# Edge chunks of seven in place of four in a four-layer graph network on one core

## The reference

```python
# conv: batch norm over the edges, gate and update, sum by dst
z = concat([h[src], h[dst], edge]);  gate = sigmoid(bn(z @ W_int + b_int));  upd = softplus(bn(z @ W_upd + b_upd))
conv = softplus(h + bn(segment_sum(gate * upd, dst)))
# sage: mean of the neighbours
sage = (segment_sum(h[src], dst) / deg) @ w_l.T + h @ w_r.T + b
# hops, three times: a mask for every edge from both its ends, then a masked sum by src
a = relu([relu(x[src] @ nb_W), relu(x[dst] @ self_W)] @ att1_W + b);  mask = clip(sigmoid(a @ att2_W) * 1.5 - 0.45, 0, 1)
d = clip(rowsum(mask) ** -0.5, 0, 10);  x = segment_sum(mask * d[src] * d[dst] * x[dst], src);  out += x
# classifier: message of node and edge, mean by dst, layer norm
msg = relu([h[src], edge] @ W1 + b1) @ W2 + b2;  out = layernorm(h + segment_sum(msg, dst) / deg)
```

## Time and profile before

| | us |
|---|---|
| median of 3 runs | 15924.5 (15921.29 to 15934.76) |
| the profiled execution | 15891.89 |
| its span | 15890.3 |
| PE, DVE, ACT, POOL busy | 8863.8, 7549.7, 6748.7, 5861.8 |
| stages in their order: placing, conv spread, statistics, messages | 3215, 967, 1034, 1099 |
| sage's sum; first masks; first hop; one spread | 742; 863; 747; 240 |
| classifier's spread; its sum | 446; 715 |

### The profile page before, as it was taken

How to read it: one execution, slowest core, us unless ns; L and a number is a source line. 1 busy time by engine, 2 the same in 40 slices (tenths; PEclk the granted TensorE clock), 3 DMA queues, 4 the chain that set the end, 5 groups by cost and what they waited for, 6 DMA issues and landing times. The chain is left out here.

```text
span 15890.3 us, 411251 instructions
## 1 busy us (share of the span) xinstructions
PE 8863.8 (56%) x144293; PEld 8049.9 (51%) x144294; DVE 7549.7 (48%) x15637; ACT 6748.7 (42%) x18309; POOL 5861.8 (37%) x5933
## 2 busy tenths in 40 slices
PE   6444444447755578756664454654544644545755
PEld 6444444447755567754554454544544544544634
DVE  4333333347689988614416614346334166143044
ACT  0111111128866678660062276642566622765500
POOL 2444444435510001016415426235156155163065
PEclk9995555559987789775586675776755866756955
DMA  3222221018877678674375574665755755745954
GB/s 133 65 69 65 65 65 49 17 47 318 315 223 203 198 225 257 195 263 160 105 275 173 165 283 159 191 237 179 254 183 158 257 174 172 274 159 152 329 164 131
DMA packets 1136260, 2824.13 MB, mean 178 GB/s; under 512 B 381504, under 2 KB 524864, under 8 KB 1013954
## 3 DMA queue, kind: packets, MB, share of 16 engines
q1 hardware_dynamic: 841198, 2073.90, 38.0%
q0 software_dynamic: 294592, 747.67, 16.4%
q10 hardware_dynamic: 276, 0.01, 0.0%
HBM read 1738.10 MB, written 1023.06 MB: 174 GB/s over the span
## 5 line engine op out<-in xcount | busy, mean ns | idle before, releaser
L496 POOL DMA_INDIRECT rows_s<-place_rec,place_index x1568 | 1524.9, 973 | 1868.4 <-DVEq L615 1203.1
L1884 POOL DMA_INDIRECT mask_cols<-cols_all,mask_index x1368 | 1319.4, 964 | 2092.1 <-ACT mask_index L1891 1732.5
L2022 POOL DMA_INDIRECT hop_x<-cols_all,hop_index x1368 | 1380.4, 1009 | 1726.5 <-ACT hop_index L2029 1404.4
L2078 PE MATMUL hop_sums_ps<-hop_parts,hop_onehot 128*128 128x64 bf16 x16416 | 1078.5, 238 | 1193.0 <-issue 850.3
L2078 PEld LDWEIGHTS hop_sums_ps<-hop_parts,hop_onehot 128*128 128x128 bf16 x16416 | 913.7, 127 | 1360.0 <-issue 1356.7
L2054 DVE TENSOR_TENSOR hop_parts<-hop_parts 128x512 f32<-128x512 f32 x684 | 475.2, 695 | 1981.1 <-ACT hop_parts L2038 1063.6
L507 ACT COPY place_oh_turned<-place_turn_ps 100x1024 bf16<-100x1024 bf16 x197 | 199.4, 1012 | 2825.4 <-remote 1914.5
L2038 ACT ACTIVATE hop_parts<-hop_x,mask 128x64 f32<-128x64 f32 x5472 | 1376.0, 334 | 35.5 <-issue 35.4
L1967 DVE TENSOR_TENSOR mask_hidden<-mask_part_ps,mask_cols 128x512 f32<-128x512 f32 x684 | 470.4, 688 | 1638.0 <-DMA cm_v<-rows_all 686.9
L532 PE MATMUL place_same_ps<-place_oh_turned 100*128 100x128 bf16 x1568 | 197.7, 307 | 1661.5 <-ACT place_ohd_turned L508 1202.0
L150 ACT COPY mask_now<-row_part 128x192 bf16 x1368 | 411.1, 348 | 1612.0 <-DMA cm_v<-rows_all 1316.7
(11 more groups left out here) (382 smaller groups left out, 27373.6 us busy)
## 6 DMA issues: line engine op xcount, KB each, us to landing
cols_all<-att_in_rows SPq DMA_DIRECT2D x171, 1024.0 KB
mask_onehot<-hot_s SPq DMA_DIRECT2D x171, 1024.0 KB
cols_all<-hop_in_rows SPq DMA_DIRECT2D x171, 1024.0 KB
hop_onehot<-hot_s SPq DMA_DIRECT2D x171, 1024.0 KB
rows_all<-blank SPq DMA_DIRECT2D x76, 1551.0 KB
ct_u<-rows_all SPq DMA_DIRECT2D x228, 517.0 KB
cm_v<-rows_all SPq DMA_DIRECT2D x228, 512.0 KB, 3.6
cm_onehot<-hot_d POOLq DMA_DIRECT2D x228, 512.0 KB
```

The source lines that it names most:

```text
L496: nc.gpsimd.indirect_dma_start(m.rows_s.rearrange("p n w -> (p n) w"), bass.IndirectOffsetOnAxis(index[:, j, t:t + 1], 0), rec[:, j, t, :] ...
L1884: nc.gpsimd.indirect_dma_start(cols[:, s * 4 + i, b, :], None, table, bass.IndirectOffsetOnAxis(index[:, s * 4 + i, b:b + 1], 0)).then_inc ...
L2022: nc.gpsimd.indirect_dma_start(x[:, s * 4 + i, b * C:(b + 1) * C, :].rearrange("p c f -> p (c f)"), None, table, bass.IndirectOffsetOnAxis ...
L2078: last = nc.tensor.matmul(block_of(sums, blocks[t // C]), onehot[:, s, i, t, :], upper(parts[:, i, q, t * F:(t + 1) * F]), start=False, st ...
```

## The change

C is 7, NBT is 288, and an iteration is one batch: IT = 288, BATCH = 7. There are 2016 edge slots of 128 in place of 1824. Whatever came twice an iteration comes once: the copy of a block's parts, the indirect DMA (rows of 1792 bytes, in conv's scatter 3616), the sum collected into `acc`. PSUM tiles keep room for 8 slots. In placing, shifts and masks by 4 turn into a product with 1/7 rounded by adding and taking off 12582912. In conv's spread DVE copies four edges of `u` and ACT three, where each had four. In the messages DVE multiplies the message of this iteration before the older sum, and adds the other end of the next iteration last. The classifier's spread loads `e_turned` and stores `cols_all` in quads (896 KB) with three buffers. Loops' unrolling and look-aheads stay.

```diff
-C = 4
-NBT = 456
+C = 7
+NBT = 288
...
-IT = NBT // 2
-BATCH = 2 * C
+IT = NBT
+BATCH = C
...
-NBS = 460
+NBS = 300
 T = NBT * C
+SPLIT = 4
+WHOLE = 12582912.0
...
-QR = 4
+QR = 3
...
     def copy(self, it, i):
         blocks = self.blocks.of(it, i)
-        for b in range(2):
-            last = self.nc.scalar.copy(self.now[:, i, b, :, :], self.parts[:, bass.ds(blocks[b], 1), :, :].rearrange("p a q f -> p (a q) f"))
-        last.then_inc(self.staged, 1)
+        self.nc.scalar.copy(self.now[:, i, :, :], self.parts[:, bass.ds(blocks[0], 1), :, :].rearrange("p a q f -> p (a q) f")).then_inc(self.staged, 1)
...
-                        s.mark(nc.vector.tensor_single_scalar(chunk, at, 2, ALU.logical_shift_right))
-                        s.mark(nc.vector.tensor_single_scalar(batch, at, 9, ALU.logical_shift_right))
-                        s.then(nc.vector.tensor_single_scalar(edge, at, C - 1, ALU.bitwise_and))
+                        s.then(nc.vector.tensor_scalar(seventh[:], at, 1.0 / C, -(C - 1) / 2 / C, ALU.mult, ALU.add))
+                        s.then(nc.vector.tensor_scalar(chunk, seventh[:], WHOLE, WHOLE, ALU.add, ALU.subtract))
+                        s.mark(nc.vector.tensor_single_scalar(batch, chunk, 7, ALU.logical_shift_right))
+                        s.then(nc.vector.scalar_tensor_tensor(out=edge, in0=chunk, scalar=-float(C), in1=at,
+                                                              op0=ALU.mult, op1=ALU.add))
...
-                    for b in range(2):
-                        nc.gpsimd.indirect_dma_start(rows_d, bass.IndirectOffsetOnAxis(index[:, i, b:b + 1], 0),
-                                                     u[:, i, b, :], None).then_inc(scattered[i], 16)
+                    nc.gpsimd.indirect_dma_start(rows_d, bass.IndirectOffsetOnAxis(index[:, i, :], 0),
+                                                 u[:, i, :], None).then_inc(scattered[i], 16)
...
-                    nc.vector.tensor_copy(u[:, i, 1, 0:C * W].rearrange("p (t f) -> p t f", f=W),
-                                          u_ps[i % 2][:, C:BATCH, :]).then_inc(taken_v, 1)
+                    nc.vector.tensor_copy(u[:, i, 0:SPLIT * W].rearrange("p (t f) -> p t f", f=W),
+                                          u_ps[i % 2][:, 0:SPLIT, :]).then_inc(taken_v, 1)
...
-                    nc.scalar.copy(u[:, i, 0, 0:C * W].rearrange("p (t f) -> p t f", f=W), u_ps[i % 2][:, 0:C, :]).then_inc(taken_a, 1)
+                    nc.scalar.copy(u[:, i, SPLIT * W:C * W].rearrange("p (t f) -> p t f", f=W), u_ps[i % 2][:, SPLIT:C, :]).then_inc(taken_a, 1)
...
                     if ahead:
                         rescale(it + 8, (n + 8) % 12, k + (n + 8) // 12)
-                    open_up(it, s, i, k)
+                    weigh(it, s, i, k)
                     if collects:
-                        collect(it - 1, (i - 1) % 4, 0, order)
+                        collect(it - 1, (i - 1) % 4, order)
                     if ahead:
                         value(it + 8, (n + 8) % 12)
-                    weigh(it, s, i, k)
-                    if collects:
-                        collect(it - 1, (i - 1) % 4, 1, order)
+                    if more:
+                        open_up(it + 1, (n + 1) // 4 % 3, (n + 1) % 4, k + (n + 1) // 12)
...
-        e_turned = sb("e_turned", [P, 4, BATCH, P], bf16)
-        rows = sb("rows", [P, 4, 2, C * F])
+        e_turned = sb("e_turned", [P, 3, 4, BATCH, P], bf16)
+        rows = sb("rows", [P, 3, 4, BATCH, F])
...
-                    sp.wait_ge(taken, it + 5)
-                    sp.dma_start(m.cols_all[:, bass.ds(it * 2, 2), :], rows[:, i, :, :]).then_inc(written[i], 16)
-                    if look_ahead(it, 4):
-                        sp.wait_ge(spread, it + 1)
-                        load_e(it + 4, i)
-                        if i == 3 and look_ahead(it, 12):
+                    if i == 3:
+                        sp.wait_ge(taken, it + 5)
+                        sp.dma_start(m.cols_all[:, bass.ds((k * 3 + s) * 4, 4), :],
+                                     rows[:, s, :, :, :].rearrange("p i (b c) f -> p (i b) (c f)", c=C)).then_inc(written[s], 16)
+                        if look_ahead(it, 12):
+                            sp.wait_ge(spread, it + 1)
                             load(k * 3 + s + 3, s)
...
-                    for b in range(2):
-                        nc.gpsimd.indirect_dma_start(x[:, s * 4 + i, b * C:(b + 1) * C, :].rearrange("p c f -> p (c f)"), None, table,
-                                                     bass.IndirectOffsetOnAxis(index[:, s * 4 + i, b:b + 1], 0)).then_inc(arrived[s * 4 + i], 16)
+                    nc.gpsimd.indirect_dma_start(x[:, s * 4 + i, :, :].rearrange("p c f -> p (c f)"), None, table,
+                                                 bass.IndirectOffsetOnAxis(index[:, s * 4 + i, :], 0)).then_inc(arrived[s * 4 + i], 16)
...
```

239 lines of the change are left out of this document (114 added, 125 removed).

## The result

The changed kernel takes 14384.1 us (median of 4 runs, 14368.2 to 14404.3) against 15922.9 before: a ratio of 0.903, 95% interval 0.9017 to 0.9042. The profiled execution took 14380.2 us (span 14378.1), 1511.7 less than the profiled one before. The forecast was 14950, its range 14320 to 15650; the result lies inside it, 64 us above its low end, close to rival B's 14340 and 566 us from the forecast.

What follows compares the result with a forecast made beforehand. No engine bounds the whole; in the gather stages, 40% of the span, POOL's issuing and PE's instruction supply collide. Gathers -1280 and other terms +301 make -979 from 15892, 14913, plus 33 for the median: 14950 us, range 14320 to 15650.

Steps and rivals of the forecast that it cites:

- rival B: Gather stages: PE's collision with POOL's gathers goes, stages fall to the next engine; -1888 us there, 14340 total; chance 0.25.
- Taken off: 1.26 us in hops and masks: Hops and masks: one gather fewer saves its pitch of 1.26 us an iteration; -166 us each hop, -128 each mask.
- 2x1.26 + 0.75: Hop, kernel before: an iteration is two gather pitches plus PE's own time, 3.27 us.
- the floor of 430 us for PE in sage's sum: Sage's sum: PE's 28 matmuls of 53 ns an iteration allow no less than 430 us.
- so I add 20: 1005: Messages: DVE 950, PE 968 and DMA 983 us lie together, so 20 is added: 1005 us, -50.
- DMA's 0.81x1099x1.105 = 983: Messages: DMA's busy share of the stage, scaled by the 10.5% more slots, gives 983 us.
- at the 367 GB/s that the plain spreads reach: Classifier's spread: larger transfers at 367 GB/s against 330 would give 443 us; taken as 457, +11.
- The doubt about the Trainium skill's rule on batching to a MiB: Classifier's spread: the rule alone overstates the gain, since short transfers already reach 330 GB/s with many in flight.
- Rival C: Gather stages: PE's stall belongs to the iteration, so dropping a gather returns only 0.65 us; 16380 total; chance 0.08.
- Its second form: Gather stages: a 1792-byte gather costs by its bytes, 1.75 of one, saving only 0.3 us and ending slower.
- Rival D: Gather stages: part of a gather's time is covered, so it is worth 1.0 us; -651 us, 15580 total; chance 0.15.
- A: The forecast itself, gather stages: a gather costs exactly its pitch; -1280 us, 14950 total; chance 0.50.

Runs made afterwards that it cites:

- experiment 1: Changed kernel with spare gathers added in the hops, in one of four, two of four and every iteration: hops 624, 734, 936 us against 519; whole 15115 us.
- experiment 3: Changed kernel with one small spare gather more per hop iteration (16 rows, 128 short rows, 64 rows): hops 922, 921, 923 us; whole 15595 us.
- experiment 5: Changed kernel with every second gather left out in both sums: sage's sum 381 us against 533, classifier's 377 against 501.
- experiment 6: Changed kernel with old message order and small classifier-spread transfers: 14791 us; kernel before with new order and 1 MB transfers: 15745 us.
- experiment 7: Changed kernel with a spare second gather per hop iteration and 7, 14, 21 matmuls: hops 796, 802, 797 us; separately, with pauses in both sums: 13070 us.

## Why the prediction was right or wrong

| term | predicted | measured, profiled executions |
|---|---|---|
| placing | +20 | +22 |
| conv's spread | +15 | +11 |
| statistics | +130 | +120 |
| messages | -50 | -138 |
| seven spreads | +175 | +160 |
| classifier's spread | +11 | -33 |
| hops | -498 | -685 |
| masks | -384 | -533 |
| the two sums | -398 | -420 |
| rest (starts and ends of stages, products of nodes) | 0 | -16 |
| sum | -979 | -1512 |

(Measured in either trace from a stage's first matmul of the loop to its last, the messages from the first of the spread to the last of the sums.)

The direction, and that the gather stages decide it, were right, for the reason given: a gather fewer a chunk, at a price that does not grow with its row. The terms of the full stages came within 15 us. Placing's +22 is no check of its +20: the stage took 3203 to 3214 us in the three traces with the old kernel's placing and 3207 to 3243 in the seven with the new, on the slower kind of chip. That the total came inside the range is in part luck: gather stages, messages and classifier's spread all gave more than forecast. It would not have come so on the quicker kind of chip, where the change takes off 402 us and not 979. Off were these steps.

*"Taken off: 1.26 us in hops and masks".* This is where most of the error is. The step took a gather's cost from POOL's pitch. The cost is 1.45 to 1.5 us per issue in a hop (experiments 1 and 3), so a hop falls by 0.2 us more an iteration, 58 us each: 523 in place of 581, against 519 measured, 1.80 us an iteration where ACT's pace is 1.76. The forecast made 3.27 us of 2x1.26 + 0.75 and gave the 0.75 to PE's own time; experiment 1 says it is 2x1.45 + 0.35. The pitch itself was read low: the five steps of the earlier trace rows from 9598.34 to 9604.79 are 1.29 us each. The row for it was there: the last gather of a burst ends, and PE is slow for some 0.9 us more, which is no part of any pitch.

*Rival B*, that the collision goes and the stages fall to the next engine, is what hops (518 predicted, 519 measured) and masks (655, 671) did. The corrected price gives nearly the same there, 523 and (3.78 - 1.46)x288 = 668; that the next engine's floor is reached, and not only this price paid, shows in the quicker chips' 511 and 665 us without any hold-up. The two sums did what the forecast said (545 and 514; 533 and 501) and not B (450, 430). It was not one mechanism everywhere. The line is whether the next engine's iteration is longer than what a gather costs: ACT's 1.76 us in a hop and DVE's 2.2 in the masks are, DVE's 1.31 in the sums is not. In the sums half the gathers bring the 377 to 381 that would be the floor (experiment 5). B's total is near by an offset: its gather stages gave 1888 us and the measured ones 1638, 250 less, while the other terms came 174 us under their +301. And the floor of 430 us for PE in sage's sum, in B and in the forecast, was taken at the lower clock: the stage went to 381 in experiment 5 and 405 on a quicker chip.

*Messages, "so I add 20: 1005".* Two things were wrong. The 1005 was held against 1055, the length of the sums alone, while its largest term, DMA's 983, was worked out from the whole 1099; against 1099 the same working gives -94. And the bound itself, DMA's 0.81x1099x1.105 = 983, did not come: DMA's busy time did not grow with the bytes, 0.93x960 = 893 us against 0.81x1099 = 890, at 310 GB/s in place of 245. The share of busy time had been read as work to be scaled by bytes, and it isn't: it was 0.80x1273 = 1018 us with the same bytes in the old order (experiment 6). What else it holds no run shows. The reorder was right and worth 103 to 313 us by the number of batches (experiment 6); without it the chunks of seven would have made this term +175.

*Classifier's spread, "at the 367 GB/s that the plain spreads reach".* It reaches 394 (397 with chunks of four); it reads more for each byte that it writes than they do, and whether that is why no run shows. Larger transfers in deeper buffers gave 76 to 115 us. The doubt about the Trainium skill's rule on batching to a MiB ("DMA: Bandwidth & Descriptors", Bandwidth) went too far: the trace before had 330 GB/s with 256 KB transfers, but 397 was to be had with 1 MB ones. That agrees with the rule's direction, if size and not depth did it, and the 341 GB/s that the page gives for one megabyte alone is exceeded with several in flight.

*Rival C*, half a pitch returned, has nothing for it: no term came out under its pitch. Its second form (a gather by its bytes) is refuted by experiment 3.

*Rival D*, a gather worth 1.0 us, is refuted on the first kind of chip. On the quicker kind it is nearer than A: by experiment 7 a hop's gather is worth 2.77 - 1.78 = 1.0 us there. If the other terms are as in the table, the gather stages gave back some 402 + 126 = 528 us there, where D has 651 and A 1280. This is an estimate, since no trace of the kernel before was taken on such a chip.

## What to carry to other kernels

An indirect DMA costs by the issue: 16 rows of 1792 bytes and 128 rows of 256 cost the same, 1.45 us right behind another one on the first kind of chip. So bring down their number, by longer rows and at the price of padding, until the next engine's iteration is longer than the issue's cost (what still longer rows would do was not tried); then price what the padding adds in the stages that are full. When a loop goes from two units to one an iteration, look for waits that the second unit had covered: the order in DVE's loop was worth 103 us before and 313 after. A price taken from one chip's trace may hold for that chip alone; where "issue" and "remote" waits stand high, time both versions on several.

## What the runs showed of the hardware that was not expected

The same kernel took two times, a sixth apart, and no time between: the kernel before 15912 to 15935 us on some chips (9 and 12 among them) and 13287 to 13332 on others (13 and 3), the changed one 14384 and 12910; the change is worth 9.7% on the first kind and 3.0% on the second. All slower runs came before all quicker ones, so that it is the chip, and not something else that changed between, is likely but not shown. What differs is what runs beside POOL's indirect DMAs: on the first kind PE gets one or two matmuls through in 0.7 us while they are issued back to back, and placing has 2017 us of "remote" waits; on the second PE keeps its 62 ns a matmul in a hop and there are no such waits. The gathers themselves take nearly the same in the changed kernel, 0.95 to 1.09 us in the mean of a stage on the first and 0.95 to 1.03 on the second. The stages without many gathers or scatters agree: statistics 1149 us on both, a plain spread 262 to 265. What lies behind this, and why PE is held up while ACT and DVE keep their 334 and 630 ns an instruction, no run here shows. The kernel before was timed but not traced on the quicker kind, so how the change's 402 us split there is not shown either. For a hop there is an estimate from experiment 7: two gathers at 1.38 us each make 2.77 us an iteration, 631 us for 228 iterations, some 120 us above the 511 of the changed kernel.
